# Two of six hidden tiles of a gated feed-forward layer multiplied on GpSimd, and the int8 input widened there

## The reference

```python
def _act_fake_quant(x, clip_factor):
    scale = jax.nn.sigmoid(clip_factor) * jnp.max(jnp.abs(x)) / QMAX
    return jnp.clip(_ste_round(x / scale), -QMAX - 1.0, QMAX) * scale
...
xq = _act_fake_quant(x, clip_x[0])
gate = jnp.einsum('bsh,ih->bsi', xq, _weight_fake_quant(w_gate))
up = jnp.einsum('bsh,ih->bsi', xq, _weight_fake_quant(w_up))
h = _act_fake_quant(jax.nn.silu(gate) * up, clip_down[0])
return jnp.einsum('bsi,hi->bsh', h, _weight_fake_quant(w_down))
```

## Time and profile before

| | us |
| --- | --- |
| runs (3) | 1474.04, 1475.9, 1478.81; median 1475.9 |
| profiled execution | 1475.61 |
| its span in the trace | 1473.6 |
| input half of the feed-forward layer, first silu to last maximum | 1348.19 to 1415.09 |
| one batch of it, silu of tile 0 to the next silu of tile 0 | 8.1 to 8.15 |
| GpSimd busy in it | 0 |

### The profile page before, as it was taken

The page is one execution under the profiler, slowest core; times in us unless marked ns, Lnnn a source line. Parts: engine busy times, 40 slices in busy tenths (PEclk is TensorE's granted clock), DMA queues, the critical chain, the costliest instruction groups (busy, mean ns, idle before and its releaser), DMA issues. The chain is left out here.

```text
span 1473.6 us, 30046 instructions
## 1 busy us (share of the span) xinstructions
PE 1290.3 (88%) x8705; PEld 996.1 (68%) x8710; DVE 1039.8 (71%) x2788; ACT 767.6 (52%) x1940; POOL 553.1 (38%) x834
## 2 busy tenths in 40 slices
PE   4989989998964799999999999999999999944866
PEld 2867877787842577777777777777777788731223
DVE  5566666656554777787877778868877877763986
ACT  3222223232221566666766766666767676624853
POOL 1333332333322675444444344444444444510004
PEclk9999999999986799999999999999999999976987
DMA  6232211220205300001000000010010000202115
GB/s 227 70 118 101 72 57 71 100 83 15 74 31 177 100 16 2 2 2 30 2 30 4 2 30 2 2 32 2 1 30 2 16 2 2 74 15 61 57 57 172
DMA packets 51043, 71.55 MB, mean 49 GB/s; under 512 B 4497, under 2 KB 43665, under 8 KB 48850
## 3 DMA queue, kind: packets, MB, share of 16 engines
q1 hardware_dynamic: 50338, 69.60, 14.3%
q10 hardware_dynamic: 560, 0.20, 0.1%
HBM read 57.07 MB, written 12.72 MB: 47 GB/s over the span
## 5 line engine op out<-in xcount | busy, mean ns | idle before, releaser
L837 POOL TENSOR_SCALAR scores<-scores,att_rinv 128x128 f32<-128x128 f32 (+3 forms) x512 | 264.3, 532 | 204.4 <-DVE att_rinv L1049 204.4
L893 ACT ACTIVATE scores<-scores,att_top 128x128 f32<-128x128 f32 (+3 forms) x512 | 281.5, 553 | 89.2 <-DVE att_top L1031 88.9
L1031 DVE CUSTOM_DVE_ANT_0 scores<-ps_y,w_bias_b,null_s 128x128 f32<-128x128 f32 x448 | 229.4, 547 | 100.5 <-PE ps_y L1181 89.1
L261 POOL TENSOR_TENSOR act_w<-act_g,wide_w 128x512 f32<-128x512 f32 x64 | 105.5, 1649 | 282.9 <-DVE act_g L379 277.4
L1192 PE MATMUL ps_up<-ident,scores 128*128 128x128 f32 x1280 | 191.7, 274 | 8.2 <-DVE keep L1059 6.2
L1180 PE MATMUL ps_y<-k_hh,q_hl 128*128 128x256 f32 (+2 forms) x512 | 187.6, 376 | 12.8 <-DVE att_top L1031 5.9
L1202 PE MATMUL ps_a<-keep,w_val 128*64 128x128 f32 x2560 | 197.2, 284 | 0.3 <-DVE keep L1059 0.3
L901 ACT ACTIVATE keep<-ps_up 128x128 f32<-128x128 f32 (+3 forms) x256 | 111.9, 437 | 156.1 <-PE ps_up L1192 153.2
L208 ACT ACTIVATE hid_hi<-hid 128x512 fp32r<-128x512 f32 x80 | 50.5, 631 | 241.8 <-DVE hid L397 241.7
L1192 PEld LDWEIGHTS ps_up<-ident,scores 128*128 128x128 f32 x1280 | 150.3, 140 | 30.9 <-issue 10.4
L844 POOL TENSOR_SCALAR w_q_hm<-q_hl 64x512 fp32r<-64x512 f32 x128 | 76.7, 612 | 239.0 <-ACT q_hl L916 239.0
(11 more groups left out here) (236 smaller groups left out, 2594.6 us busy)
## 6 DMA issues: line engine op xcount, KB each, us to landing
wide_w<-token_w_dram SPq DMA_DIRECT2D x16, 1024.0 KB, 4.7
x_raw<-in_x_t_dram SPq DMA_DIRECT2D x8, 512.0 KB, 3.7
x_nat<-in_x_nat_dram SPq DMA_DIRECT2D x8, 512.0 KB, 4.7
x_dram<-x_nat SPq DMA_DIRECT2D x8, 512.0 KB, 2.9
w_x1t<-x_dram SPq DMA_DIRECT2D x8, 512.0 KB, 4.0
c_dram<-out_raw SPq DMA_DIRECT2D x8, 512.0 KB, 3.2
c2t<-c_dram SPq DMA_DIRECT2D x8, 512.0 KB, 3.7
x_tile<-x_dram SPq DMA_DIRECT2D x8, 512.0 KB, 4.4
```

The source lines that it names most:

```text
L261: nc.gpsimd.tensor_tensor(act_w[:, k % 2], act_g[:, k % 2], wide_w[:, k], ALU.mult).then_inc(sem.act_w_ready, 1)
L837: nc.gpsimd.tensor_scalar(s, s, rinv[:, pp, q, hh:hh + 1], 0.0, ALU.mult, ALU.add).then_inc(sem.p_normed, 1)
L893: nc.scalar.activation(s, s, ACT.Exp, scale=-1.0, bias=top[:, pp, q, hh:hh + 1], accum_out=lsum[:, pp, q, hh:hh + 1]).then_inc(sem.exp_don ...
L1031: dve.tensor_tensor_reduce(scores_of(pp, hh, q), psS[:, hh, 0:n], bias_of(w, h)[:, CAUSAL[q]:CAUSAL[q] + n], 1.0, null_s[:, par, q, h:h + ...
```

## The change

Three things are done to the input block.

1. Tiles 1 and 3 (`MIXED`) of each batch no longer go through DVE's product. ACT copies the up bank, scaled, into a new SBUF buffer `up_sb` (one buffer, function `ups`), and GpSimd multiplies that with `silu` into `hid` (function `mixed`). A new semaphore `up_ready` gives PE the up bank back, and `hid_mixed` gives ACT the silu buffer and `up_sb` back. DVE still takes the maxima of all six tiles.
2. The widening from int8 to bf16 moves from ACT to GpSimd (function `widen`). On GpSimd it stands between the products of tiles 1 and 3. ACT's quantisation now waits until the previous batch has been widened.
3. PE's `turn` moves from behind tile 2 to behind tile 3, and ACT's `turned_out` from behind the silu of tile 3 to behind that of tile 4.

The diff, cut to its core:

```diff
             def _(act):
                 def quantise(f, par):
                     act.wait_ge(sem.c2_in, 16 * (f + 1))
-                    if not known(f, 2):
-                        act.wait_ge(sem.cqt_done, f - 1)
+                    if not known(f, 1):
+                        act.wait_ge(sem.cq_ready, f)
                     nc.scalar.activation(c8[:], c2t[:, par], ACT.Copy, scale=w.x_scale[:, 1:2]
                                          ).then_inc(sem.c8_ready, 1)
-                    act.wait_ge(sem.c8_ready, f + 1)
-                    nc.scalar.activation(cq[:, par], c8[:], ACT.Copy).then_inc(sem.cq_ready, 1)
...
+                def ups(b, k):
+                    s = IC * b + k
+                    act.wait_ge(sem.fu_done, s + 1)
+                    if not known(turn_of(b, k), 2):
+                        act.wait_ge(sem.hid_mixed, turn_of(b, k) - 1)
+                    nc.scalar.activation(up_sb[0:rows(k)], ps.up[0:rows(k), k % 2], ACT.Copy,
+                                         scale=w.in_scale[0:rows(k), IC + k:IC + k + 1]).then_inc(sem.up_ready, 1)
+
                 def batch(b, par, ahead):
                     for k in range(IC):
-                        silus(IC * b + k, k)
+                        silus(b, k)
+                        if k in MIXED:
+                            ups(b, k)
                         if ahead and k == 0:
                             quantise(b + 1, 1 - par)
-                        if ahead and k == 3:
+                        if ahead and k == 4:
                             turned_out(b + 1, 1 - par)
...
+                    hidden(b, 0)
+                    if not first:
+                        largest(b - 1, 4)
+                        largest(b - 1, 5)
+                    hidden(b, 2)
+                    largest(b, 0)
+                    largest(b, 1)
+                    hidden(b, 4)
+                    largest(b, 2)
+                    hidden(b, 5)
+                    largest(b, 3)
...
+            @block.gpsimd
+            def _(pool):
+                def mixed(b, k):
+                    pool.wait_ge(sem.up_ready, turn_of(b, k))
+                    settle(pool)
+                    r = rows(k)
+                    out = hid[0:r, k, b] if isinstance(b, int) else hid[0:r, k, bass.ds(b, 1)].squeeze(1)
+                    nc.gpsimd.tensor_tensor(out, silu[0:r, k % 2], up_sb[0:r], ALU.mult).then_inc(sem.hid_mixed, 1)
+
+                def widen(f, par):
+                    pool.wait_ge(sem.c8_ready, f + 1)
+                    if not known(f, 2):
+                        pool.wait_ge(sem.cqt_done, f - 1)
+                    settle(pool)
+                    nc.gpsimd.tensor_copy(cq[:, par], c8[:]).then_inc(sem.cq_ready, 1)
+
+                def batch(b, par, ahead):
+                    mixed(b, 1)
+                    if ahead:
+                        widen(b + 1, 1 - par)
+                    mixed(b, 3)
...
                 def batch(b, par, ahead):
                     for k in range(IC):
                         products(b, k, par)
-                        if ahead and k == 2:
+                        if ahead and k == 3:
                             turn(b + 1, 1 - par)
```

More of the change, by code:

```diff
@@ L1551, in ffn_in_phase, with turn_of, two_ago @@
         silu = sb("silu", [P, 2, S])
+        up_sb = sb("up_sb", [P, S])
         turned = ps.a1[:].bitcast(BF16).rearrange("p (c s) -> p c s", c=HC)
+        MIXED = (1, 3)
+        PLAIN = tuple(k for k in range(IC) if k not in MIXED)
         def rows(k):
             return P if k < IC - 1 else IB
+        def turn_of(b, k):
+            group = MIXED if k in MIXED else PLAIN
+            return len(group) * b + group.index(k) + 1
+        def two_ago(b, k):
+            return (b, k - 2) if k >= 2 else (b - 1, k - 2 + IC)
         with nc.Block() as block:
@@ L1589, in turned_out, with silus @@
                     nc.scalar.activation(cq_t[:, par], turned, ACT.Copy).then_inc(sem.cqt_ready, 1)
-                def silus(s, k):
+                def silus(b, k):
+                    s = IC * b + k
                     act.wait_ge(sem.fg_done, s + 1)
                     if not known(s, 2):
-                        act.wait_ge(sem.ffn_hid, s - 1)
+                        act.wait_ge(sem.hid_mixed if two_ago(b, k)[1] in MIXED else sem.ffn_hid, turn_of(*two_ago(b, k)))
                     nc.scalar.activation(silu[0:rows(k), k % 2], ps.gate[0:rows(k), k % 2], ACT.Silu,
                                          scale=w.in_scale[0:rows(k), k:k + 1]).then_inc(sem.silu_ready, 1)
+                def ups(b, k):
+                    s = IC * b + k
+                    act.wait_ge(sem.fu_done, s + 1)
[3 more added lines that the diff above has]
+                                         scale=w.in_scale[0:rows(k), IC + k:IC + k + 1]).then_inc(sem.up_ready, 1)
                 def batch(b, par, ahead):
                     for k in range(IC):
-                        silus(IC * b + k, k)
+                        silus(b, k)
+                        if k in MIXED:
+                            ups(b, k)
                         if ahead and k == 0:
                             quantise(b + 1, 1 - par)
-                        if ahead and k == 3:
+                        if ahead and k == 4:
                             turned_out(b + 1, 1 - par)
@@ L1615, in _, with place, hidden @@
             def _(dve):
-                def hidden(b, s, k):
+                def place(b, k):
+                    r = rows(k)
+                    return hid[0:r, k, b] if isinstance(b, int) else hid[0:r, k, bass.ds(b, 1)].squeeze(1)
+                def hidden(b, k):
+                    s = IC * b + k
                     dve.wait_ge(sem.silu_ready, s + 1)
                     dve.wait_ge(sem.fu_done, s + 1)
-                    out = hid[0:rows(k), k, b] if isinstance(b, int) else hid[0:rows(k), k, bass.ds(b, 1)].squeeze(1)
-                    nc.vector.scalar_tensor_tensor(out=out, in0=ps.up[0:rows(k), k % 2],
+                    nc.vector.scalar_tensor_tensor(out=place(b, k), in0=ps.up[0:rows(k), k % 2],
                                                    scalar=w.in_scale[0:rows(k), IC + k:IC + k + 1],
@@ L1626, in largest @@
                     s = IC * b + k
-                    dve.wait_ge(sem.ffn_hid, s + 1)
+                    dve.wait_ge(sem.hid_mixed if k in MIXED else sem.ffn_hid, turn_of(b, k))
                     at = slice(s, s + 1) if isinstance(b, int) else bass.ds(s, 1)
-                    src = hid[0:rows(k), k, b] if isinstance(b, int) else hid[0:rows(k), k, bass.ds(b, 1)].squeeze(1)
-                    nc.vector.tensor_reduce(w.hid_max[0:rows(k), at], src, X, ALU.max, apply_absolute_value=True)
+                    nc.vector.tensor_reduce(w.hid_max[0:rows(k), at], place(b, k), X, ALU.max, apply_absolute_value=True)
                 def batch(b, first):
[L1633 to L1638, removed]
+                    hidden(b, 0)
[9 more added lines that the diff above has]
+                    largest(b, 3)
                 nc.vector.memset(w.hid_max[:], 0.0)
@@ L1644, in _ @@
                     batch(b, False)
-                largest(B - 1, IC - 1)
+                largest(B - 1, 4)
+                largest(B - 1, 5)
                 dve.drain()
+            @block.gpsimd
[3 more added lines that the diff above has]
+                    settle(pool)
+                    r = rows(k)
+                    out = hid[0:r, k, b] if isinstance(b, int) else hid[0:r, k, bass.ds(b, 1)].squeeze(1)
[11 more added lines that the diff above has]
+                    mixed(b, 3)
+                widen(0, 0)
+                batch(0, 0, True)
+                with pool.Fori(0, (B - 2) // 2) as j:
+                    batch(2 * j + 1, 1, True)
+                    batch(2 * j + 2, 0, True)
+                batch(B - 1, 1, False)
             @block.tensor
@@ L1664, in products @@
                         pe.wait_ge(sem.cqt_ready, b + 1)
-                    for n, bank, read, done in ((0, ps.gate, sem.silu_ready, sem.fg_done),
-                                                (1, ps.up, sem.ffn_hid, sem.fu_done)):
+                    for n, bank, done in ((0, ps.gate, sem.fg_done), (1, ps.up, sem.fu_done)):
                         if not known(s, 2):
-                            pe.wait_ge(read, s - 1)
+                            if n == 0:
+                                pe.wait_ge(sem.silu_ready, s - 1)
+                            else:
+                                pe.wait_ge(sem.up_ready if two_ago(b, k)[1] in MIXED else sem.ffn_hid, turn_of(*two_ago(b, k)))
                         for c in range(HC):
@@ L1936, in named_semaphores @@
     sem.ffn_hid = new("ffn_hid")
+    sem.up_ready = new("up_ready")
+    sem.hid_mixed = new("hid_mixed")
     sem.hid_most = new("hid_most")
```

## The result

| | before | after |
| --- | --- | --- |
| median, four runs each on the same chip | 1477.36 | 1493.99 (1493.34 to 1494.75) |
| profiled execution, its span | 1475.61, 1473.6 | 1494.31, 1492.5 |
| first silu 0 to that of the last batch | 57.07 | 68.12 |
| DVE's last maximum to the output block's scale | 0.5 | 8.05 |

The change made the kernel slower: ratio 1.0115, 95% interval 1.0093 to 1.0137. The forecast was 1492.5 in 1484 to 1502.

A forecast was written before the change was run, and what follows sets the result against it. The prediction took DVE to bound the input half before the change and a ring across engines after it. Terms of 7.4, 7.5 and 2.0 gave 16.9 us on 1475.6, so 1492.5, range 1484 to 1502.

The forecast's parts named there:

- What bounds: Input half of the feed-forward layer: DVE bounds it, busy 7.58 of 8.10 us per batch, with a short ACT stall.
- Term 1: Input half: batches go from 8.15 to 9.19 us, +7.3 over seven, plus 0.1 for the first widening: +7.4.
- the ring: Input half, silu 0 to next silu 0: dependent steps through ACT, GpSimd and PE, 9.19 us per batch.
- Term 2: Output block: GpSimd's configuration change ahead of the second partition reduction delays it, +7.5 us, bounds 0 and 7.8.
- The first configuration: Input half, ahead of GpSimd's first product: the configuration change back costs 0, bounds 0 and 1.5 us.
- Term 3: Input half: PE's pause of 2.05 us per batch lowers its clock in two or three of eight batches, +2 us.
- The free second configuration: Output block: the configuration ahead of the second reduction costs nothing, giving 1485 us; chance 12%.
- the slow widening: Input half: GpSimd's widening costs as much as a two-input instruction, +11.1 us, giving 1503.6; chance 11%.
- Contention: Input half: DVE holds up GpSimd's products, 0.39 us longer on eight rings, +3.1, giving 1495.6; chance 6%.
- Faster: Input half: a batch under 6.45 us, or under 7.5 without the second configuration's cost, gains over 4.4 us; chance 2%.

The follow-up runs named there:

- e4: The changed kernel with GpSimd's widening of the next batch ahead of the product of tile 1 instead of behind it: 1490.19 us (1.0097).
- e2: The kernel before plus one GpSimd product of 128x1 at the start of the input block, its output unused: 1483.41 us (1.0044).
- e5: The changed kernel with the widening back on ACT, the products of tiles 1 and 3 still on GpSimd: 1489.72 us (1.0092).
- e6: The changed kernel with six extra PE products of 512 columns per batch ahead of the turn, results unread: 1490.05 us (1.0093).
- e1: The changed kernel with the output block's partition reduction made by a PE product and a DVE maximum instead of GpSimd: 1486.63 us (1.0077).

## Why the prediction was right

- **What bounds.** Right. DVE was the bound, and the new order makes a ring in which DVE's saving is worth nothing: 6.34 busy of 9.05.
- **Term 1, the ring, +7.4.** The mechanism is right, by the releasers above and by e4: with the widening out of the ring a batch takes 8.10. The length was 9.19 by my sum, 9.06 by the trace, so seven batches gave 6.4. The pieces: the copy of up takes 0.68 from PSUM with a scale, not 0.59, but the next instruction starts 0.57 behind it; handover and register work took 0.24, not 0.32; product 1.26 for 1.28, with the widening starting 0.05 before its end; widening 1.04 for 1.06. The turn's pause was 1.88 for 2.05. The last batch gave -0.1 for 0, the first widening's handover 0.1 as said.
- **Term 2, the second configuration, +7.5.** Measured 7.6 in the trace, and 7.25 in e2 by itself. The Trainium skill (GPSIMD Engine Reference, section 2.1, Instruction dispatch) gives about 6 us (5.95) for a first call into a library; the trace doesn't agree, with 7.4 to 7.6 from the record to the output block's reduction (the change, e2, e4, e5, e6) and 7.8 to 8.4 to the setup block's.
- **The first configuration, 0.** The visible cost is right (0.3), the working was not. "I take 0, since nothing in the row shows a cost" was the step that failed: the change back costs 7.0 to 8.2 as well (the change, e1, e2, e4, e6). By line and by timeline the change has

```profile
L1684 POOLq MODIFY_POOL_CONFIG  x2: 13/13/13, 1345.6 to 1345.7; - x2
...
1352.63 1.26 POOL L1684 TENSOR_TENSOR ffn_hidden<-silu,up_sb 128x512 f32<-128x512 f32 x1 [7.04 <-ACT up_sb L1613]
```

7.0 apart, and the copy that this product multiplies ended at 1352.12, 0.5 before it, where in the loop it is 0.24. All but some 0.3 us was hidden, only since it stands right behind the first widening; in e1 and e6, with it in the same place, 0.9 and 0.7 came out. Two swapped lines brought it out at its full price (e4).
- **Term 3, the clock, +2.** The mechanism is right (e6), the size was under half of what it was: I counted two or three batches at 0.8, the trace has four at 1.0 to 1.1, together 4.3 to 4.4, and e6's seven stretches are 4.1 shorter. In e1, where the batches are the same, it was six, or 6.6 us, which is more than the 6.4 that the prediction took for the worst. Which batches lose the clock differs from one program to the next, and no run shows what decides it.
- **The rest.** 0.8 came ahead of the phase, which the change doesn't touch, and -0.5 behind the reduction; I had neither. Term 1 was 1.0 too much, term 3 2.3 too little, and with the 0.3 of the first configuration that makes 2.0: the span grew by 18.9, for 16.9 forecast. The profiled execution took 1494.31, for 1492.5. The nearness of the sum owes something to errors of both signs.
- **The rivals.** The free second configuration is refuted by e2, the slow widening by its group (1037 ns). Contention is refuted here: the product's group is 1264 ns, beside DVE's products and maxima, near the 1.28 of the earlier trace rows and far from the 1.67. The Trainium skill (Perfetto Trace Analysis, Optimizing Scalar/DVE Operations) warns of the port that both share and ties the lock to a DVE operation that uses both of its ports. DVE's products here read one PSUM bank and one SBUF tile and its maxima one SBUF tile, so this group says nothing against that warning; it shows only that these instructions didn't slow GpSimd's products. The 1.67 of the earlier trace rows, beside a DVE instruction with two SBUF operands, would fit it, but no run varies that. "Faster" failed where it was said to: product and widening together need 2.3 in the ring.

## What to carry to other kernels

An engine that gets work taken off it must be the one that the others wait for in the new order too: walk the new order once around the loop, instruction by instruction, before counting what was taken off. Before a helper engine is given work, look which of its instructions stand on each side, since in these programs a product on GpSimd between two partition reductions brings a change of configuration each way; the casts here brought none. If a stall is filled by moving one part (the widening), measure that part alone, because it may be the whole of the gain.

## What the runs showed of the hardware

- The change of GpSimd's configuration takes 7.0 to 8.4 us from its record to the next instruction, in both directions: 7.4 to 8.4 to the partition reduction, 7.0 to 8.2 back to a TENSOR_TENSOR. It has no busy time, is booked as "issue" or as whatever else came last, and runs beside other engines' work: it costs nothing where the next instruction isn't due sooner.
- CAST of int8 to bf16 (128x1024) took 1.04 us on GpSimd, nearly what ACT needs for it (1.06), and needed no change of configuration behind a reduction.
- Where PE paused for 1.88 us in each batch, the granted clock fell in four of seven batches in one program (to 0.57 over 3.4 us of one of them) and in six of seven in another. Where the pause in the same place was 0.60 (e6), or no pause was longer than 0.96 (e5), it stayed at 1.00 behind the first batch.
- The maximum over 128 partitions by PE and DVE took 1.26 us from input to scale, where the reduction on GpSimd takes 0.49 with its configuration ready and 8.05 without.
